# A decoder layer in fp32: order of the scans, the weightings and a few low parts in the first and the last batches

## The reference

```python
# 1: linear attention with gates; 8 heads of 64
h = x * rsqrt(mean(x * x) + 1e-6) * norm_w
q, k, v = rope(h @ Wq.T), rope(h @ Wk.T), h @ Wv.T
f, g, o = sigmoid(h @ Wbeta.T + bbeta), sigmoid(h @ Wig.T + big), sigmoid(h @ Wog.T + bog)
M = M * f[t] + g[t] / 8 * outer(k[t], v[t])        # for each token t, from M = 0
y[t] = (q[t] @ M) * o[t]
x = layernorm(x + y @ Wout.T + bout)
# 2: a memory of the context, r = 0.9 * r + ctx[t] ** 2
x = layernorm(x + x * r[t])
# 3: eight experts; each takes 128 of the 1024 tokens of a micro batch, of which there are 4
xn = norm(x) * gamma + beta
x = layernorm(x + gelu(xn @ w1[e] + b1[e]) @ w2[e] + b2[e])
```

## Time and profile before

| what | value |
|---|---|
| median of three runs | 1304.98 us (1303.05 to 1307.32) |
| the profiled execution, its own time | 1301.37 us |
| its span | 1299.6 us |
| mean granted clock of TensorE | 0.992 |
| busy: PE, PEld | 1269.3 us (98%), 1032.9 us (79%) |
| busy: DVE, ACT, POOL | 730.2 us (56%), 460.3 us (35%), 754.7 us (58%) |
| DMA | 172.08 MB, 132 GB/s in the mean |

### The profile page before, as it was taken

The page is one execution under the profiler, slowest core; times in us unless marked ns, Lnnn a source line. Parts: engine busy times, 40 slices in busy tenths (PEclk is TensorE's granted clock), DMA queues, the critical chain, the costliest instruction groups (busy, mean ns, idle before and its releaser), DMA issues.

```text
span 1299.6 us, 19475 instructions
## 1 busy us (share of the span) xinstructions
PE 1269.3 (98%) x6850; PEld 1032.9 (79%) x6850; DVE 730.2 (56%) x1269; ACT 460.3 (35%) x629; POOL 754.7 (58%) x519
## 2 busy tenths in 40 slices
PE   8889999999999999889999999999999999999998
PEld 7668888888888888768888888888788888888886
DVE  5688888888887888862343333343333423433324
ACT  5223332333333332443433434433434335344330
POOL 4766666667666666537537456274284376364551
PEclk9989999999999999989999999999999999999999
DMA  8666666666666664527207125135053071071210
GB/s 281 157 148 150 156 151 152 153 155 154 154 146 159 144 156 106 178 90 242 74 1 266 65 82 186 65 133 199 2 185 147 1 266 67 18 249 65 88 74 33
DMA packets 132612, 172.08 MB, mean 132 GB/s; under 512 B 13692, under 2 KB 75980, under 8 KB 132556
## 3 DMA queue, kind: packets, MB, share of 16 engines
q1 hardware_dynamic: 132556, 171.30, 45.8%
HBM read 137.44 MB, written 17.05 MB: 119 GB/s over the span
## 4 chain that ended last, share of the span: by engine, by line
PE 92%; DVE 3%; issue 2%; POOL 1%; DMA 1%; ACT 1%; SPq 0%; POOLq 0%; DVEq 0%
PE qk_ps L86 9%; PE qk_ps L88 9%; PE qk_ps L87 9%; PE v_ps L86 7%; PE v_ps L88 6%; PE v_ps L87 6%; PE gate_ps L86 5%; PE gate_ps L87 5%; PE gate_ps L88 5%; PE y_ps L86 3%; PE y_ps L87 3%; PE y_ps L88 3%; PE s_ps L86 3%; PE s_ps L88 3%; PE s_ps L87 3%; PE turn L1359 2%
## 5 line engine op out<-in xcount | busy, mean ns | idle before, releaser
L937 POOL TENSOR_TENSOR w_lo<-w_raw,w_hi 128x2048 fp32r<-128x2048 f32 x31 | 143.4, 4626 | 73.1 <-ACT w_hi L707 73.1
L929 POOL TENSOR_TENSOR w_lo<-w_raw,w_hi 128x2048 fp32r<-128x2048 f32 x32 | 148.0, 4625 | 15.8 <-ACT w_hi L717 15.8
L1015 DVE TENSOR_TENSOR_SCAN decays<-f_all,diag 128x384 f32<-128x384 f32 x128 | 150.3, 1214 | 0.6
L86 PE MATMUL qk_ps<-xT_parts,wqkv_hi 128*128 128x256 f32 x512 | 149.6, 292 | 0.9 <-DVE wqkv_lo L974 0.8
L1208 DVE CAST hid_hi<-gate_ps 128x512 fp32r<-128x512 f32 x62 | 42.9, 692 | 189.8 <-ACT gate_ps L741 189.6
L88 PE MATMUL qk_ps<-xT_parts,wqkv_lo 128*128 128x256 f32 x512 | 144.8, 283 | 0.0
L87 PE MATMUL qk_ps<-xT_parts,wqkv_hi 128*128 128x256 f32 x512 | 144.5, 282 | 0.0
L1208 DVE CAST hid_hi<-v_ps 128x512 fp32r<-128x512 f32 x62 | 42.9, 692 | 175.5 <-ACT v_ps L741 175.5
L901 POOL TENSOR_TENSOR rstd_b<-mean_var_b,ln_eps_b 128x4 f32<-128x4 f32 x15 | 3.7, 245 | 213.2 <-DVE mean_var_b L1193 213.2
L847 POOL TENSOR_TENSOR rot<-rot 128x256 f32<-128x256 f32 x64 | 70.3, 1099 | 95.9 <-DVE rot L1042 93.2
L741 ACT ACTIVATE gate_ps<-gate_ps,b_cols 128x512 f32<-128x512 f32 x64 | 42.2, 659 | 190.8 <-PE gate_ps L88 190.8
(11 more groups left out here) (228 smaller groups left out, 3175.4 us busy)
## 6 DMA issues: line engine op xcount, KB each, us to landing
w_raw<-in_w SPq DMA_DIRECT2D x64, 1024.0 KB, 7.5
f_all<-f_dram SPq DMA_DIRECT2D x16, 1024.0 KB, 4.8
qkT<-rot SPq DMA_DIRECT2D x256, 64.0 KB, 2.0
xT_raw<-in_xT SPq DMA_DIRECT2D x16, 512.0 KB
x_both<-in_x SPq DMA_DIRECT2D x16, 512.0 KB
f_all<-f_dram SPq DMA_DIRECT2D x16, 512.0 KB, 6.0
c_both<-in_ctx_in SPq DMA_DIRECT2D x16, 512.0 KB, 11.9
x_dram<-res SPq DMA_DIRECT2D x16, 512.0 KB, 12.5
```

The source lines that it names most:

```text
L86: eng.matmul(out, lhs_hi, rhs_hi, start=first, stop=False)
L929: pool.tensor_tensor(w2_lo[s % 2][:], w2_raw[s % 2][:], w2_hi[s % 2][:].bitcast(F32), ALU.subtract)\
L937: pool.tensor_tensor(w1_lo[s % 2][:], w1_raw[s % 2][:], w1_hi[s % 2][:].bitcast(F32), ALU.subtract)\
L1015: dve.tensor_tensor_scan(decays[:, n, :], f_all[:, n, :], diag[:], 0.0, ALU.mult, ALU.add).then_inc(decay_done, 1)
```

## The change

The order of a few instructions is changed in step 0 and 1 and in the steps 15 to 17; nothing is computed in another way, and no instruction is added or taken away.

- VectorE, batch 0: its scans 2 and 3 go from step 1 to the end of step 0, ahead of the first weighting; 4 and 5 stay behind it.
- VectorE, batch 1: scans 2 and 3 stay ahead of the last weighting of batch 0, scans 4 to 7 come later; 5, 6 and 7 now stand at the end, ahead of the residual.
- VectorE, batch 15: scans 4 to 7 come later, the last of them behind two `token_low`; in step 16 the first weighting comes ahead of the statistics, the second ahead of `add_memory`, the third ahead of the second statistics.
- GpSimd, step 0 and 1: `out_weights_low` comes behind the rms scale of batch 2 and waits for all scans of batch 0; then `residual(1)`, `x_low(2)`; `context_low(0)` comes behind the first two rotations.
- GpSimd, step 16: `context_low(15)` waits for `add_memory(14)` and comes first; `split_w2` of the first slab comes behind the norm's scale.
- ScalarE: the squares of the context of batch 0 come one y_high later, those of batch 15 ahead of the high part of the first w2 slab.
- SyncE: in step 1 it waits until the rows `f_all` of batch 1 have landed (both DMAs) before it stores the rms values of batch 2 and loads x, its transpose and the context.

VectorE's `body` is written anew as straight lists, one per kind of step (`first`, `second`, `middle`, `behind`); for the steps 2 to 14 they give the order of before. The core of the diff:

```diff
@@ SyncE, body
+                if b.n == 1:
+                    sp.wait_ge(f_in, 32 * 2)
                 if (b + 1).within(B):
                     store_rms(b + 1)
@@ ScalarE, body
-                    if b.n == 1 and c == 0:
+                    if b.n == 1 and c == 1:
                         square_ctx(b - 1)
...
                 if b.n == B - 1:
+                    square_ctx(b)
                     split_w2(Step(0), 0)
-                    square_ctx(b)
@@ GpSimd, body
                 if (b + 1).within(B):
                     rms_scale(b + 1)
+                    if b.n == 1:
+                        pool.wait_ge(decay_done, NH)
+                        out_weights_low()
+                        residual(b)
                     if b.n >= 1:
                         x_low(b + 1)
                 if b.n == B:
-                    split_w2(Step(0), 0)
+                    pool.wait_ge(u_done, (b - 2).after(NT, NT))
+                    context_low(b - 1)
                 if (b - 2).within(B):
                     norm_scale(b - 2)
-                if b.n == 1:
-                    residual(b)
-                if (b - 1).within(B):
+                if b.n == B:
+                    split_w2(Step(0), 0)
+                if 2 <= b.n <= B - 1:
                     context_low(b - 1)
...
                     rotate(b, 1)
+                if b.n == 1:
+                    context_low(b - 1)
...
                     residual(b)
-                    out_weights_low()
@@ VectorE, the new lists
+            def behind(b):
+                weigh_pair(b, 0)
+                norm_stats(b - 1, 0)
+                weigh_pair(b, 1)
+                add_memory(b - 1)
+                y_low(b, 0)
+                weigh_pair(b, 2)
+                y_low(b, 1)
+                norm_stats(b - 1, 1)
+                weigh_pair(b, 3)
+                y_low(b, 2)
+                split_hidden(Step(0), 0)
+                y_low(b, 3)
+                split_hidden(Step(0), 1)
```

More of the change, by code:

```diff
@@ L1152, in body, with weigh_pair, scans @@
+            def weigh_pair(b, c):
+                weigh(b, 2 * c)
+                weigh(b, 2 * c + 1)
+            def scans(b, *heads):
+                for n in heads:
+                    scan(b, n)
+            def body(b):
                 if b.n == -1:
@@ new lines, in middle @@
+            def middle(b, last):
+                add_memory(b - 2)
+                norm_stats(b - 2, 1)
+                weigh_pair(b - 1, 0)
+                weigh_pair(b - 1, 1)
+                token_gates(b)
+                gate_v(b, 0)
+                y_low(b - 1, 0)
+                rope_parts(b, 0)
+                clear_f(b)
+                scans(b, 0, 1)
+                weigh_pair(b - 1, 2)
+                if last:
+                    token_stats()
+                    token_means()
+                y_low(b - 1, 1)
+                rope_parts(b, 1)
+                scans(b, 2, 3)
+                if not last:
+                    scans(b, 4, 5)
+                weigh_pair(b - 1, 3)
+                gate_v(b, 1)
+                y_low(b - 1, 2)
+                rope_parts(b, 2)
+                scans(b, 4 if last else 6)
+                y_low(b - 1, 3)
+                rope_parts(b, 3)
+                if last:
+                    scans(b, 5, 6)
+                    add_residual(b - 1, 0)
+                    token_low(Step(0), 0)
+                    token_low(Step(0), 1)
+                    scans(b, 7)
+                    add_residual(b - 1, 1)
+                    token_low(Step(0), 2)
+                    token_low(Step(0), 3)
+                else:
+                    sum_gates(b + 1)
+                    scans(b, 7)
+                    add_residual(b - 1, 0)
+                    add_residual(b - 1, 1)
+                    norm_stats(b - 1, 0)
```

131 lines of the change are left out of this document (56 added, 75 removed).

## The result

| | before | after |
|---|---|---|
| median of the runs | 1306.04 us (1303.05 to 1307.32, 5 runs) | 1291.62 us (1290.52 to 1295.48, 5 runs) |
| ratio | | 0.9896 [0.9875, 0.9916] |
| the profiled execution | 1301.37 us | 1291.02 us |
| its span | 1299.6 us | 1289.2 us |
| mean granted clock | 0.992 | 0.994 |

The change makes the kernel faster: 14.4 us between the medians (the interval of the ratio leaves out 1), 10.4 between the two profiled executions. The difference of 4 between those two figures is a question of its own, which two of the experiments take up.

What follows compares the result with a forecast made beforehand. TensorE is full from 80 to 530 us; five waits for VectorE at the edges (18.2) and lost clock (8.0) leave 26 at most. First batches 4.4 plus last 3.9 give 8.3: 1304.98 becomes 1297, range 1289 to 1303.

Steps and rivals of the forecast that it cites:

- rival A: VectorE and GpSimd meet less than thought, or the clock stays up: first batches 12, last 5.4; 1285 to 1290; chance 0.15.
- Scans 2 and 3 of batch 0, priced at a new wait of 1.0: Moved into VectorE's idle 2.35, they stand behind GpSimd's addition, taking 37.7 to 39.4; TensorE waits 1.0 for the first weighting.
- The wait for v goes, f_all lands at 53.6: Batch 1: TensorE's 2.77 wait and 1.7 of clock go; f_all's second part lands 6.0 after issue, not 11.3.
- The four scans to 62.8, TensorE on at 63.9: Batch 1's scans from 53.6 meet GpSimd's moved work, ending at 62.8; TensorE goes on 6.2 sooner than 70.08.
- The alternation: Behind f_all of batch 1, VectorE and GpSimd take turns: one scan, one GpSimd instruction, the last scan ending at 62.8.
- The bound without a meeting, 58.3: First batches: with scans never blocked, TensorE would go on at 58.3, 11.8 sooner.
- VectorE's 18.5 from there to scores 1 of batch 1: Weighting to weighting: 14.0, plus 1.8 for moved scans, 2.0 behind context_low, 0.7 behind a rotation; first batches give 4.4.
- The rms values: Batch 2's, behind SyncE's new wait: 13.7 from store to use, landed 69.5, needed 70.4; price 0, 1 us of slack.
- Rival D: Slower: SyncE's wait queues rms store, loads and moves; decides once rms_rows come after 74.8; 1306 or 1310; chance 0.07.
- Rival C: f_all still lands 11.3 after issue, at 58.9; rms_rows 4.4 late, first batches give 0; 1301 to 1302.7; chance 0.11.
- Last batches, 3.9: Steps 15 to 17: scores 3 of batch 15 come 2.3 sooner, plus half of 3.1 of clock; bounds 0.5 to 5.4.
- The bound of 12 for the first batches: First batches' gain if the scans are not blocked; the sum's upper bound took 6.2 in its place.

## Why the prediction was right

Predicted 1297 (1289 to 1303), faster with 0.75; it came to 1291.62. The direction held, and the mechanism in the main; the size was 8.3 for 14.4. The 1291.62 lie under the 1293 to 1302 that the sum's own bounds gave, and inside the range only because it had been widened for rival A.

**Scans 2 and 3 of batch 0, priced at a new wait of 1.0: wrong.** They were not blocked, and TensorE didn't wait: GpSimd's addition, 0.2 ahead of them, stood in their place. My step let whoever starts first hold the other out. At scans 6 and 7 the start times agree with that, here they don't: 4.15 to 4.17 in ten kernels, each time with the addition 0.2 ahead. Why it falls the other way here stays open.

**The wait for v goes, f_all lands at 53.6: right.** The wait and its fall of the clock are gone (48 to 54 at 1.00), `f_all` came at 53.35. The rule I had weighed (the Trainium skill, "DMA: Bandwidth & Descriptors", section "Queues, rings and completion order": descriptors are consumed in ring order) can't by itself account for the 11.0 with the stores alone behind the rows; the trace is against reading a landing off it.

**The four scans to 62.8, TensorE on at 63.9: right.** 62.1 and 63.16. The alternation gave 9.2 from landing to the last scan, with a y_low between them the trace has 8.65. The bound without a meeting, 58.3, was 59.00 when GpSimd was idle. The rule of the Trainium skill ("SBUF — State Buffer", section "Who interferes with whom") is that two SBUF inputs on VectorE and a GpSimd instruction that reads SBUF exclude each other for a whole instruction. The trace agrees that they do: 0.9 a scan alone and 2.1 beside GpSimd, and 4.19 for one scan beside a 128x2048. Which of the two stands, the start times here don't settle.

**VectorE's 18.5 from there to scores 1 of batch 1: too long by 0.7.** From the start of one weighting to that of the next it was 17.8 (62.02 to 79.83), with 2.76 for the scan behind `context_low` as priced, and nothing for the rotation, which stood itself (70.11 for 3.42). It also began 0.8 sooner than the 62.8 of the sum. So no wait of 1.8, and 80.93 instead of 82.4: 5.9 of gain, not 4.4.

**The rms values: right with less than I said.** 9.9 from store to use, not 13.7, and no wait. The slack is small all the same: in the kernels that came 1 to 2 us sooner VectorE waited 3.8 and 2.5 for them. Rival D had its mechanism, with the point not reached. Rival C's late landing did come when the wait was taken out, and cost 1.6 by the medians, inside their intervals.

**Last batches, 3.9: right, 4.4 measured.** With the 5.7 that the first batches had shifted it taken off, the last scan was foreseen at 538.2 to 541.7 (538.10 for 4.19), the load of w2 at 542.5 (542.31), the waits at 1.3 and some 3 (1.45, 2.83), the memory product at 1.4 (1.41). That the sum fits so well is in part luck, since two terms were off against each other. TensorE was not 0.4 ahead at scores 1 but 0.6 behind, as the clock fell behind the 2.83, which I hadn't counted, and scores 3 came 1.6 sooner, not 2.3. And the fall of 561 to 568 went whole, not half. I had read a fall off the length of the wait (1.60 without, 1.89 with one); behind waits of 2.78 to 2.83 at this one place it came in four kernels and not in three.

**The size.** Of the 6.1 us that the forecast was short, 1.5 lie in the first batches as traced and 0.5 in the last. Another 1.1 is the median of before, 1304.98 in three runs and 1306.04 in five. The other 3 are in the base: I subtracted from the median what I had worked out against a profiled execution that lay 3.6 under it, and took the distance for a constant. Part of it was likely the matter itself. In two other executions with the old order the seam of batch 0 costs 3 to 4 more, and the change takes that away too, since no GpSimd instruction stands beside scans 6 and 7 any more. The row was there: 3.92 for two scans which alone take 1.81 was a blocked pair, and what a blocked pair costs depends on the phase. The bound of 12 for the first batches, which the sum replaced by 6.2, was the nearer one: by the medians they gave 10.0 (against the kernel with the last batches alone) to 11.5. Rival A had such a gain, but by scans that are hardly blocked, and they were blocked.

## What to carry to other kernels

Where two engines exclude each other on memory, price a stretch by who stands behind whom and place the long instruction of one where the other has work that showed no loss beside it (here products with an input in PSUM). Holding GpSimd back with a wait won 4 us at once here and left the whole 7 us slower. A profiled execution that lies apart from the median of its runs may be a luckier or unluckier one: look at its blocked instructions and ask what they would cost in another phase. Before a fall of the clock is priced, ask what would be waited for without it. And a small store, queued behind a load, can hold up the load's signal.

## What was not expected of the hardware

- GpSimd stands for VectorE too. An addition that takes 2.39 us alone took 4.16 when two scans followed 0.2 behind its start, and a rotation of 0.72 took 3.42 beside three scans. The one that stood was not the one that started later.
- A 512 KB transfer landed 11.0 us after its issue instead of 5.8 once two stores of 0.5 KB in 4-byte pieces were queued behind it, with the DMA engines idle for the last 3.5 of these.
- Behind a wait of 2.78 to 2.83 us at one place the clock fell to the lower level in four kernels and stayed at 1.00 in three. The three were only 0.2 to 1.0 us quicker than the changed kernel over that stretch; what the clock gave, a later wait took.
